# Two row buffers instead of three, and weight halves made two tiles ahead on GpSimd, in the second expert layer of a decoder kernel

## The reference

```python
def _L1_ffn_ref(x, Wg, Wu, Wd, W1, W2):      # T = 2048 tokens, D = 256, F = 512, E = 8
    probs = jax.nn.softmax(xt @ Wg, axis=-1)
    topv, topi = jax.lax.top_k(probs, 2)
    topv = topv / jnp.sum(topv, axis=-1, keepdims=True)
    cw = jnp.zeros((T, E), x.dtype).at[jnp.arange(T)[:, None], topi].set(topv)
    h = _gelu(jnp.einsum('td,edf->tef', xt, Wu))
    y = jnp.einsum('tef,efd->ted', h, Wd)
    moe = jnp.einsum('ted,te->td', y, cw)
    shared = _gelu(xt @ W1) @ W2
    return (shared + moe).reshape(B, S, D)
```

## Time and profile before

| | |
|---|---|
| median of 3 runs | 1545.79 us (1545.47 to 1549.87) |
| profiled execution | 1545.79 us, of which the span is 1543.6 us |
| busy, share of the span | PE 89%, DVE 72%, ACT 60%, POOL 54% |
| mean granted TensorE clock | 0.947 |
| transposes of tile 10 to those of tile 24 | 1380.09 to 1475.98 us: 95.89 us |
| the rest up to 1510.50, mostly the singles | 34.52 us |

### The profile page before, as it was taken

The page is one execution under the profiler, slowest core; times in us unless marked ns, Lnnn a source line. Parts: engine busy times, 40 slices in busy tenths (PEclk is TensorE's granted clock), DMA queues, the critical chain, the costliest instruction groups (busy, mean ns, idle before and its releaser), DMA issues.

```text
span 1543.6 us, 27707 instructions
## 1 busy us (share of the span) xinstructions
PE 1366.4 (89%) x9290; PEld 1103.7 (71%) x9290; DVE 1110.5 (72%) x2430; ACT 929.9 (60%) x2302; POOL 831.1 (54%) x866
## 2 busy tenths in 40 slices
PE   4787999999999999966999999878899998999991
PEld 3566777777777777745899999734556665999891
DVE  4677876766766667646588886389898995867835
ACT  4666565655655556533488884157787873457753
POOL 3655454444444444431588874148796884057740
PEclk9899999999999999975799999988999999999995
DMA  4100000000000000034566657674454331227674
GB/s 150 42 28 7 3 34 1 8 8 1 8 8 2 8 2 1 1 112 171 190 217 229 235 207 235 245 256 134 132 166 130 130 131 55 83 100 242 216 245 173
DMA packets 52942, 167.85 MB, mean 109 GB/s; under 512 B 13178, under 2 KB 22340, under 8 KB 44996
## 3 DMA queue, kind: packets, MB, share of 16 engines
q1 hardware_dynamic: 45316, 145.63, 26.9%
q0 software_dynamic: 7488, 20.46, 4.1%
HBM read 149.28 MB, written 16.78 MB: 108 GB/s over the span
## 4 chain that ended last, share of the span: by engine, by line
PE 32%; DVE 8%; POOL 7%; issue 5%; ACT 3%; DMA 1%; POOLq 0%; DVEq 0%; ACTq 0%; SPq 0%
PE m_ps L1756 9%; PE m_ps L1779 9%; POOL s_hc L2082 4%; PE m_ps L1753 2%; PE m_ps L1774 2%; PE s_yps L2517 2%; DVE s_h L2452 2%; PE m_ps L1736 1%; DVE tokens L1624 1%; DVE m_hs L1552 1%; ACT s_dps L2161 1%; PE m_ps L1704 1%; PE m_ps L1660 1%; DMA table<-m_xn 0%; PE m_ps L1715 0%
## 5 line engine op out<-in xcount | busy, mean ns | idle before, releaser
L306 POOL TENSOR_TENSOR a_pexp<-a_pexp,a_rsum 128x384 f32<-128x384 f32 (+1 forms) x320 | 246.1, 787 | 302.7 <-DVE a_rsum L523 302.7
L396 ACT ACTIVATE a_pexp<-a_ps,a_nmax 128x384 f32<-128x384 f32 (+1 forms) x320 | 180.8, 565 | 171.5 <-DVE a_nmax L519 170.9
L519 DVE TENSOR_REDUCE a_nmax<-a_ps 128x1 f32<-128x384 f32 (+1 forms) x320 | 153.9, 522 | 71.3 <-PE a_ps L620 70.2
L2082 POOL TENSOR_TENSOR s_hc<-s_h,s_bc_rows 128x1024 f32<-128x1024 f32 x64 | 151.0, 2361 | 55.9 <-DVE s_h L2452 55.5
L1756 PE MATMUL m_ps<-m_xT,m_w1s 128*128 128x256 f32 x1032 | 156.9, 290 | 4.4 <-DVE m_xT L1509 4.4
L1779 PE MATMUL m_ps<-m_w2s,m_hs 128*128 128x256 f32 x1032 | 154.1, 286 | 4.5 <-DVE m_hs L1552 3.7
L1103 POOL DMA_INDIRECT m_xrow<-table,m_row_from x78 | 84.4, 1082 | 121.7 <-DVE m_row_from L1451 85.7
L2452 DVE TENSOR_TENSOR_SCAN s_h<-s_dps,s_inp 128x512 f32<-128x512 f32 x128 | 148.8, 1204 | 0.0
L636 PE MATMUL a_ps<-a_ident,a_pexp 128*128 128x128 f32 x896 | 144.3, 274 | 3.4 <-ACT a_pT L255 3.0
L1756 PEld LDWEIGHTS m_ps<-m_xT,m_w1s 128*128 128x128 f32 x1032 | 138.6, 195 | 5.1 <-DVE m_xT L1509 4.8
L1779 PEld LDWEIGHTS m_ps<-m_w2s,m_hs 128*128 128x128 f32 x1032 | 136.6, 192 | 6.4 <-ACT m_yrow L1238 3.4
(11 more groups left out here) (442 smaller groups left out, 3572.9 us busy)
## 6 DMA issues: line engine op xcount, KB each, us to landing
s_bc_rows<-s_bc_table SPq DMA_DIRECT2D x64, 512.0 KB, 3.7
arrived<-in_down SPq DMA_DIRECT2D x29, 1024.0 KB, 6.2
arrived<-in_up SPq DMA_DIRECT2D x23, 1024.0 KB
m_w<-in_up SPq DMA_DIRECT2D x16, 512.0 KB
m_w<-in_down SPq DMA_DIRECT2D x16, 512.0 KB
carried_up<-in_up SPq DMA_DIRECT2D x8, 512.0 KB, 5.8
carried_down<-in_down SPq DMA_DIRECT2D x8, 512.0 KB, 7.8
arrived<-results SPq DMA_DIRECT2D x3, 1024.0 KB, 8.5
```

Source lines behind the costliest of these rows:

```text
L306: nc.gpsimd.tensor_tensor(pexp[:, r, 0:n], pexp[:, r, 0:n], rsum[:, r:r + 1].to_broadcast([128, n]), ALU.mult).then_inc(normed, 1)
L396: nc.scalar.activation(pexp[:, r, 0:n], ps_s[score_bank(u)][:, 0:n], ACT.Exp, bias=nmax[:, r:r + 1], accum_out=sums[:, r:r + 1]).then_inc( ...
L519: nc.vector.tensor_reduce(nmax[:, u % RING:u % RING + 1], ps_s[score_bank(u)][:, 0:keys_of(u)], AX.X, ALU.max, negate=True).then_inc(maxed, 1)
L2082: nc.gpsimd.tensor_tensor(halves(hc[:, u % HC_RING, :]), halves(h[:, u % H_RING, :]), bc_rows[:, u % BC_RING, 1, :].unsqueeze(1).to_broadc ...
```

## The change

The row buffers of the second expert layer go from three to two. A gather is issued three tiles ahead instead of four, and waits for the transposes two tiles before its own. GpSimd's low half is made for tile j + 2 in the loop of tile j, where it was made for tile j + 1; two tiles instead of one are handled before the loop. The tile `bcast` (2 KB a partition) is allocated in both layers, also in the second, where nothing uses it; it takes the bytes that the third row buffer leaves. In the first expert layer X_BUFS was 2 and LOOK is 1, so all its expressions keep their values.

```diff
-    X_BUFS = 3 if shared else 2
...
-        if ln_rows is not None:
-            bcast = sb("bcast", [128, 2, D])
+        bcast = sb("bcast", [128, 2, D])
...
-        xrow = sb("xrow", [128, X_BUFS, 2, D])
+        xrow = sb("xrow", [128, 2, 2, D])
...
             def gather_rows(j):
-                b = j % X_BUFS
-                pool.wait_ge(xT_raw, j + 3 - X_BUFS)
+                b = j % 2
+                pool.wait_ge(xT_raw, j + 1)
...
-            for n in range(2, X_BUFS + 1):
-                gather_rows(TILES_SHARED + n)
+            gather_rows(TILES_SHARED + 2)
             if shared:
-                for c in range(FT):
-                    low_part(TILES_SHARED, c)
+                for n in range(LOOK):
+                    for c in range(FT):
+                        low_part(TILES_SHARED + n, c)
             for j in range(TILES_SHARED, TILES):
-                if j + X_BUFS + 1 < TILES:
-                    gather_rows(j + X_BUFS + 1)
+                if j + 3 < TILES:
+                    gather_rows(j + 3)
                 if shared and j == TILES_SHARED + 1:
                     destinations()
                 for c in range(FT):
-                    if j + 1 < TILES:
-                        low_part(j + 1, c)
+                    if j + LOOK < TILES:
+                        low_part(j + LOOK, c)
                     if c == FT // 2 and j > TILES_SHARED:
                         scatter_rows(j - 1)
...
             def transposes(j):
-                b = j % X_BUFS
+                b = j % 2
                 if routed(j):
-                    pe.wait_ge(xrow_loaded[b], transfers(j, X_BUFS))
+                    pe.wait_ge(xrow_loaded[b], transfers(j, 2))
```

More of the change, by code:

```diff
@@ L953, in moe_layer @@
         s_var = sem("s_var"); s_rstd = sem("s_rstd"); s_double = sem("s_double")
-        xrow_loaded = [sem(f"xrow_loaded{b}") for b in range(X_BUFS)]
+        xrow_loaded = [sem(f"xrow_loaded{b}") for b in range(2)]
         up_loaded = [sem(f"up_loaded{b}") for b in range(W_BUFS)]; down_loaded = [sem(f"down_loaded{b}") for b in range(W_BUFS)]
```

## The result

The changed kernel takes 1560.5 us (median of 5 runs, 1557.93 to 1561.37) against 1546.63 for the kernel before (median of 5, 1545.47 to 1551.16). The ratio is 1.0078, with a 95% interval of 1.0055 to 1.0100: about 12 to 14 us slower, where 1541.3 was predicted.

What follows compares the result with a forecast made beforehand. TensorE was taken as the bound, held up by up to 1.8 us in every two tiles. The sum was 1545.8 - 5.0 (collisions) + 0.2 (first half) + 0.3 (tile 13's gather) = 1541.3 us, range 1537 to 1548.5.

Steps and rivals of the forecast that it cites:

- The gain: Second expert layer, even tiles: moving GpSimd's low half removes seven collisions with VectorE's low half, gaining 5.0 us (bounds 0 and 8.4).
- forecast gap: VectorE's idle time behind ScalarE's high half, where GpSimd's moved low half should fit with 0.2 to 0.5 us to spare.
- The rival that VectorE's long low half isn't GpSimd's doing: VectorE's half starts first, so something in its own order delays it; moving GpSimd's half does nothing, 1545.8 us; chance 0.10.
- 7.37 + x: Least time for two tiles: gather starts 7.37 us after even-tile transposes and lands x later; x taken as 5.4 us.
- hidden up to x = 5.7: Even-tile gathers landing within 5.7 us of starting cost TensorE nothing; at the assumed 5.4, 0.3 us was to spare.
- TensorE itself needs 13.1: Two tiles of the second expert layer take TensorE 14.28 - 1.17 = 13.1 us once the collision is gone.
- the smaller waits: In the second expert layer ScalarE sees some `up` groups late; these waits, some tenths, were taken to stay.
- The entry: Entering the steady rhythm, `destinations` (2.7 us) delays tile 13's gather; its transposes late by 0 to 0.8 us, 0.3 taken.
- late-gather rival: Gathers land late at even tiles' transposes; two tiles take 15.2 us, 0.9 more, seven times: about 1552 us; chance 0.15.
- the 8.4 us: TensorE's whole idle time from tile 10 to 24: seven windows make 95.89 us against 87.5 at 12.5 each.
- Singles: 0: In the singles each gather has one part and about 5 us before it is wanted, so the shorter lead costs 0.
- The first half's new collision: GpSimd's very first low half, some 2.4 us earlier after tile 10's gather, meets another VectorE half: 0.2 us, bounds 0 and 1.2.

Runs made afterwards that it cites:

- half ahead of the scatter: Kernel before with one line moved: for odd tiles GpSimd makes the next tile's low half before the scatter instead of behind it; 1543.24 us, ratio 0.9973.
- calm session: First session of follow-up runs, in which none of the four profiles shows TensorE stopping without a visible releaser; the kernel before took 1533.2 us there.
- loads cut: Second expert layer's weight loads cut from 1024 to 384 KB a tile from tile 11: changed kernel 1558.96 us (1.0072), kernel before 1547.38 us (0.9996).
- three buffers: Changed kernel with three row buffers instead of two, gathers still three tiles ahead and low half two ahead; 1562.36 us, ratio 1.0087.
- half two ahead alone: Kernel before with only GpSimd's low half moved to two tiles ahead; 1533.62 us, ratio 1.0001, and in a later session 1555.82 us, 1.0042.
- both padded ones: VectorE makes chunk 3 of every even weight number three times: with only GpSimd's half moved two ahead 1556.37 us (1.0071), in the changed kernel 1561.13 us (1.0108).
- the wait alone: Kernel before, GpSimd only waiting for ScalarE's high half of two tiles ahead where the changed kernel makes its low half; no work moved; 1550.81 us, 1.0014.
- the two with the gather put ahead of the waiting half: Changed kernel, even tiles' next gather issued before GpSimd's low half: 1546.74 us (0.9985); also with `destinations` ahead of the tile loop: 1548.35 us (0.9991).

## Why the prediction was wrong

**The gain was right in place, and in size where the rest of the queue is left alone.** The half went into the forecast gap and VectorE's low half fell to 0.68 us. The half ahead of the scatter has the same without a new wait in front of a gather, and is 4.2 us faster (interval 1.5 to 6.7 us), where 5.0 was summed. Its scatters and weight loads move too, so not all of the 4.2 need be the collisions. The gain holds for a session like that one; in the calm session the collisions cost nothing. The rival that VectorE's long low half isn't GpSimd's doing has fallen: the start order stayed with VectorE first in the earlier trace rows, and moving GpSimd's half ended it. By the Trainium skill (SBUF — State Buffer, Who interferes with whom) the order of issue decides who is blocked; the recorded starts in the earlier trace rows don't show that order, while the page's statement that the two contend agrees with the runs: wherever a half of GpSimd and one of VectorE overlap, VectorE's ends about 0.56 us behind GpSimd's.

**The first step that failed is the gather's price, "7.37 + x" with x = 5.4, "hidden up to x = 5.7".** The 7.37 was good: the first issue came 6.92 us behind the transposes two tiles before for tile 16, and 7.43 for tile 18. x was 7.08 and 6.67, near the loaded bound of 7.8 and not near the idle gather that I chose it by. A gather issued together with a pair of weight loads is not an idle one: with the loads cut, only one wait of 1.1 us was left. At those x two tiles take 14.0 and 14.1 us, so in these pairs the late gather gave back the gain. The cover was mis-sized too. "TensorE itself needs 13.1" took the smaller waits for fixed; the floor is 12.3 (2 x 6.16), so that even x = 5.4 would not have hidden in the calm session. In all, late rows cost 4.8 us where 0.3 was summed.

**The entry was under-priced.** "0.3, at most 0.8" for tile 13 was 1.22, and tile 14, for which nothing was charged, waited 1.30: its gather was issued 9.43 us behind the transposes of tile 12, since the first half held GpSimd for 9.42 us and `destinations` and the scatters stood behind it. That pair took 15.21 us.

**The second step that failed, and the larger one, is "the smaller waits (ScalarE sees some `up` groups late) stay".** The late signals were counted as some tenths that no change moves, and the interruptions that go with them had no term in the sum. They make 2.9 us of stops and 4.3 us of low clock, 7 of the 10.9 us, most of it in the two long windows, and they carry the result out of the range. In the kernel before, the latest gelu came 3.4 us behind the end of its group; in the changed kernel it came 6.3 us behind. In the calm session, without them, the changed kernel lost 6.5 us; elsewhere 10 to 14.

**The late-gather rival was summed too low.** "0.9 more than now, seven times" takes all seven windows for 14.28 us, while they make 95.89. By the rival's own 15.17 they would make 106.2, 10.3 us more, and the time 1556 and not 1552. That the measured 106.81 is near this is luck: the windows were not seven of 15.2, and more than half of the loss was another thing.

**What of the late signals and interruptions is shown.** In the calm session each gelu that ScalarE was idle for starts 0.04 us behind the recorded end of its `up` group, 15 of 15 in each of the four profiles. In each of the 16 other profiles 7 to 15 such gelus start over 0.3 us behind it. This holds for every kernel, that of before too, and with the weight loads cut. It is a state that the same chip had in one session and not in another. What differs between kernels is the longest: 2.5 to 3.9 us in the six in which GpSimd does not wait for the half two ahead, 4.1 to 6.5 us in the ten in which it does. Stretches at the low clock from tile 11 on are in nine of these ten and in none of the six. The timed runs agree with the profiles. Their mean granted clock is 0.0021 to 0.0037 below that of the kernel before in the same session for the changed kernel, with three buffers, the half two ahead alone, both padded ones and the wait alone. (It is 0.0012 below with the loads cut, no more than kernels of the calm session differ among themselves.) For the two with the gather put ahead of the waiting half it is not below at all, though one of them has a low stretch in its profile. In the program these two differ from the others in what GpSimd does next behind the waiting half: a scatter, and not a gather. The half ahead of the scatter has that too. So in these runs the interruptions go with a wait for ScalarE that has a gather right behind it. No run was made to test that.

**What is open.** Late rows (half two ahead alone), the buffers, the weight traffic and dense work (padded) are each excluded as the cause. So is the fetch of instructions as far as the trace shows it: none of its DMA packets lies between 1439 and 1449, around the first stop. Whether TensorE's groups really end later than recorded, or end in time and are signalled late, can't be told, since their ends are modelled. Why a wait on GpSimd should lengthen this is not shown either. Short stops, 1.6 us in all, also occur with all low halves on VectorE, where neither wait nor collision is left, and take back part of the 8.4 us that the earlier trace rows seemed to offer.

**Smaller steps.** "Singles: 0" held (34.52 us both times), and so did "buffers and `bcast`: 0" (three buffers gave nothing back). The first half's new collision cost nothing that shows.

## What to carry to other kernels

Before work with a wait is moved forward in an in-order queue, price everything that then stands behind it by its loaded duration, and look first for a place in the same queue at which the wait is already over: here one line in front of a scatter gave what the larger change aimed at. Take the cover of a hidden transfer from the engine's floor and not from its present pace, since the pace contains the very stalls that are to go. Compare the start of an engine that waited with the recorded end of what it waited for: a distance that is 0.04 us in one session and some microseconds in another is a delay of its own, and it was written off as small here. Where a kernel's time differs by 1% between sessions, repeat a comparison in another session before it is believed; the half two ahead was level in one and 0.4% slower in the next.

## What the runs showed of the hardware

- The same kernel on the same chip took 1533.2 us in one session and 1546.3 in another. The difference lies where TensorE is dense: with all low halves on VectorE the doubles took 86.29 us and then 92.41 (medians 1536.36 and 1543.36), with two buffers only 87.28 and then 98.05 (medians 1535.41 and 1545.76; the 98.05 is from an execution of 1549.31 us).
- Outside the calm session ScalarE begins late behind the recorded end of a TensorE group that it waits for, at the worst of each profile by 2.5 to 6.5 us. In the calm one it is always 0.04 us, at a higher DMA rate (258 GB/s over the doubles against 224 in the earlier trace rows).
- A gather of two parts of 128 rows took 5.8 to 7.1 us from its first issue to its transposes beside a pair of 512 KB loads, against 5.0 at most in the earlier trace rows.
- Colliding VectorE low halves of up to 2.35 us cost TensorE next to nothing in the calm session, and 5.0 us where `up` results came late as well: what a stall on a second engine costs depends on the slack that the session leaves.
